# A post-norm decoder layer on one core: VectorE's order inside a round of the token-expert stage

## The chip, the cores and the metric

The kernel runs on one core of a Trainium2 chip as one launch. Its time is the device time in microseconds, and the lower is the better. A core has TensorE (matrix products and transposes, results in PSUM), VectorE, ScalarE, GpSimd, and SyncE, which here only issues transfers. Each engine works through a queue of its own; they meet at semaphores. In the profile PE is TensorE, PEld its weight loads, DVE VectorE, ACT ScalarE and POOL GpSimd.

## The reference

B = 4 sequences of S = 256 tokens with D = 256 features, 1024 tokens in all. Three blocks, each followed by a residual sum and a layer norm without scale or bias:

```python
x = _layernorm(x + attention(x))          # 16 heads, causal
x = _layernorm(x + xattn(x, itok, ctx))   # expert picked by the token's number
x = _layernorm(x + ffn(x))                # expert picked by a router, 4 x 1024 hidden features

def xattn(x, ids, W):                     # ctx_2048 is Wg, Wu and Wd at once: 4 matrices of 256 x 256
    e = minimum(clip(ids, 0, 12499) // 3125, 3)
    g = silu(x @ W[e].T); u = x @ W[e].T
    return (g * u) @ W[e].T

def layernorm(x): return (x - mean(x)) / sqrt(var(x) + 1e-5)
```

The change lies in the middle block. Since Wg and Wu are one matrix there, one projection z serves both: h = silu(z) z.

## The kernel before, in words

Matrix products keep nearly full float32 accuracy with three float16 products each: every operand is split into a high part (ScalarE rounds it to float16) and a low part (VectorE subtracts the high part from the original). `three` (L1099 to L1104) issues high by high, high by low and low by high for each slice of 128 features, so a product with 256 features takes six matmuls.

After attention, GpSimd scatters the 1024 normalised rows into a table in main memory sorted by expert. The four groups are padded to whole tiles of 128 rows, NS = 11 tiles in all, and SyncE loads the tiles back into `XS`. The token-expert stage then goes over them. It is a software pipeline written out by hand: all engines run through rounds s = 0, 1, 2, ..., and in round s each engine does its step for a different tile. These are the steps, with the tile each is for in round s:

- tile s: TensorE transposes the rows (L1322), ScalarE copies the high part (L595), VectorE makes the low part (L977, the first low part).
- tile s-1: TensorE makes the gate projection z (`three`, PSUM bank 2), ScalarE takes silu (L602), VectorE multiplies it by z (L991, the gate product, into `hh`).
- tile s-2: TensorE transposes h (L1341), ScalarE copies the high part (L608), VectorE makes the low part (L999, the second low part).
- tile s-3: TensorE makes the down projection (`three`, banks 4 and 7 in turn), VectorE adds the residual (L984, into `res`), takes the statistics (L995) and from them mean and variance (L1003, the means). GpSimd then adds epsilon (L443) and takes the power -0.5 (L444, into `rstd`).
- tile s-4: VectorE normalises the row (L1007, into `X2`).
- tiles s-5 and s-6: TensorE transposes `X2` (L1358), ScalarE copies it (L615), and TensorE computes the router's four logits (L1368).

TensorE's order in a round is: transpose of tile s, gate projection, transpose of h, down projection, transpose of `X2`, logits. The gate projection in round s waits for the first low part of tile s-1 and for the gate product of tile s-2, both VectorE's work of round s-1. The transpose of h also waits for the second low part of the tile before, and the down projection waits for its own second low part. Every wait is a semaphore count: `a2lo` for the first low part, `h2` for the gate product, `h2lo` for the second low part, `y2` for the down projection, `mv2` for the means, `rs2` for `rstd`, `x2_rdy` for the normalised row.

Rounds 0 to 10 take in a tile; rounds 11 to 16 drain the pipeline. The router works in two parts, tiles 0 to 6 and 7 to 10. At the start of round 13 VectorE's work for the first part is in front of the round's steps (`logits`, `top_expert`), at the start of round 14 the rest of it (`top_weight`, `places`), which ends with the rows' positions in a second sorted table (L778). From then on GpSimd scatters the eleven tiles (L451), and the last stage, the routed experts, begins when all are written. That stage has the same pair of means (L1051) and normalisation (L1056) with GpSimd's two steps between them (L457, L459).

ScalarE and VectorE also split weights for the last stage. In every second round from round 3 ScalarE takes one such chunk before its other steps (L480), so round 3 cannot start before that chunk's transfer has landed.

Of the kernel before, what the change touches and what calls it, by code (L numbers as in the profile page):

```python
# [13 lines left out]
ALU, ACT, AX = mybir.AluOpType, mybir.ActivationFunctionType, mybir.AxisListType  # L14

P = 128
B, S, D = 4, 256, 256
# [7 lines left out]
NS = NT + E - 1  # L25
# [34 lines left out]
def build(nc, x_tok, xT, ids, wqkvT, woT, ctxT, Wr, br, Wf, out):  # L60
    ctx = ExitStack()
    with ctx:
# [57 lines left out]
        mv = sb("mv", [P, 2, 2], F32)  # L120
# [42 lines left out]
        X2 = carve([NS, ROW], F32)  # L163
# [511 lines left out]
        def _(dve):  # L675
# [290 lines left out]
            for s in range(NS + 6):  # L966

                for part, (_, last) in enumerate(PARTS[:-1]):
                    if s == last + 6:
                        logits(part)  # L970
                        top_expert(part)
                    elif s == last + 7:
                        top_weight(part)
                        places(part)
                if s < NS:
                    dve.wait_ge(a2hi, s + 1)
                    v.tensor_tensor(a_lo[s % 2], ps[:, 0, 0:D].rearrange("p (k t) -> p k t", k=NK),  # L977
                                    a_hi[s % 2], ALU.subtract).then_inc(a2lo, 1)
                j = s - 3
                if 0 <= j < NS:  # L980
                    dve.wait_ge(y2, j + 1)
                    if j >= 2:
                        dve.wait_ge(x2_rdy, j - 1)
                    v.scalar_tensor_tensor(out=res[j % 2], in0=ps[:, (4, 7)[j % 2], 0:D], scalar=inv,  # L984
                                           in1=XS[:, j, 0:D], op0=ALU.mult, op1=ALU.add).then_inc(r2, 1)
                i = s - 1
                if 0 <= i < NS:
                    dve.wait_ge(sg2, i + 1)
                    if i >= 1:
                        dve.wait_ge(h2T, i)  # L990
                    v.scalar_tensor_tensor(out=hh[:, 0:D], in0=ps[:, 2, 0:D], scalar=inv, in1=sg[:, 0:D],  # L991
                                           op0=ALU.mult, op1=ALU.mult).then_inc(h2, 1)
                if 0 <= j < NS:
                    dve.wait_ge(r2, j + 1)
                    v.bn_stats(st[:, j % 2, :], res[j % 2]).then_inc(bn2, 1)  # L995
                i = s - 2
# [4 lines left out]
                if 0 <= j < NS:  # L1001
                    dve.wait_ge(bn2, j + 1)
                    v.bn_aggr(mv[:, j % 2, :], st[:, j % 2, :]).then_inc(mv2, 1)  # L1003
                i = s - 4
                if 0 <= i < NS:
                    dve.wait_ge(rs2, i + 1)
                    v.tensor_scalar(X2[:, i, 0:D], res[i % 2], mv[:, i % 2, 0:1], rstd[:, i % 2:i % 2 + 1],  # L1007
                                    ALU.subtract, ALU.mult).then_inc(x2_rdy, 1)

            last = len(PARTS) - 1  # L1010
            logits(last)
# [494 lines left out]
```

## Time and profile before

| | before |
|---|---|
| median of 3 runs | 321.65 us (321.32 to 321.87) |
| the profiled execution's own time | 322.61 us |
| its span, first to last instruction | 320.8 us |
| PE busy | 248.8 us, 78% of the span |
| DVE busy | 185.1 us, 58% |
| ACT busy | 130.3 us, 41% |
| POOL busy | 73.9 us, 23% |
| chain that ended last, by engine | PE 54%, DVE 16%, issue 9%, ACT 7%, DMA 5%, POOL 5% |

The shares are averages over stages with different limits. In time the span falls into attention (to about 131 us), the exchange of rows (to about 142 us), the token-expert stage (to about 186 us), the second exchange (to about 208 us) and the routed experts. "Idle before" in a row of a timeline is the time in which the engine did nothing before that instruction, and the releaser behind the arrow is what ended it. The duration of a row is of one instruction; neighbours on one engine overlap by some hundredths of a microsecond, so the distance from start to start is the cost of an instruction in a full queue.

### The profile page before, as it was taken

How to read it: one execution, taken by the hardware profiler on the slowest of the kernel's cores; microseconds unless marked ns; L12 is line 12 of the kernel's file. 1: busy time of each engine (PE TensorE's matmuls, PEld its weight loads, DVE VectorE, ACT ScalarE, POOL GpSimd, SP SyncE). 2: the span in 40 equal slices, each digit the busy share in tenths (PEclk: the TensorE clock that was granted, in tenths of full speed). 3: DMA queues.
4: the chain of work that ended last, by engine and by line, in shares of the span. 5: the costliest groups of instructions: out<-in, count | busy, mean ns of one | idle time of the engine just before them, and what ended most of it. 6: DMA issues, size and time to landing. Idle time of an engine off the chain costs nothing.

```text
span 320.8 us, 5861 instructions
## 1 busy us (share of the span) xinstructions
PE 248.8 (78%) x1991; PEld 165.2 (52%) x1992; DVE 185.1 (58%) x406; ACT 130.3 (41%) x218; POOL 73.9 (23%) x125
## 2 busy tenths in 40 slices
PE   4795789887986773447797537679999999999990
PEld 3364556555664551124676432236666656666570
DVE  3868577776889447813776758023544445455441
ACT  4451565855946674305575300033323213333210
POOL 8400000100141303810333268100222111222222
PEclk9799699999999998596999556599999999999997
DMA  6999072422253741448200011240000000000000
GB/s 201 339 326 284 6 261 68 127 73 67 68 164 84 215 133 39 191 144 298 102 3 0 2 42 68 89 115 2 16 18 1 2 11 16 16 16 16 9 13 2
DMA packets 18055, 29.29 MB, mean 91 GB/s; under 512 B 2796, under 2 KB 13550, under 8 KB 18032
## 3 DMA queue, kind: packets, MB, share of 16 engines
q1 hardware_dynamic: 16592, 25.81, 26.4%
q0 software_dynamic: 1440, 3.17, 2.7%
q8 instruction: 15, 0.25, 0.3%
q14 instruction: 8, 0.07, 0.1%
HBM read 19.69 MB, written 10.03 MB: 93 GB/s over the span
## 4 chain that ended last, share of the span: by engine, by line
PE 54%; DVE 16%; issue 9%; ACT 7%; DMA 5%; POOL 5%; SPq 3%; POOLq 0%; ACTq 0%; DVEq 0%
PE ps L1103 34%; DVE arena L848 3%; PE ps L1408 3%; ACT wf_hi L480 3%; PE ps L1213 2%; PE ps L1174 2%; PE ps L1109 2%; POOL sorted L422 2%; POOL sorted L451 2%; SPq L335 2%; DMA ring<-wqkvT 1%; PE ps L1170 1%; DVE wf_lo L686 1%; DVE arena L845 1%; DMA arena<-Wf 1%
## 5 line engine op out<-in xcount | busy, mean ns | idle before, releaser
L1103 PE MATMUL ps<-wf_hi,arena 128*128 x336 | 82.0, 329 | 2.8 <-DVE arena L1031 1.6
L1103 PE MATMUL ps<-wf_lo,arena 128*128 x168 | 55.2, 328 | 0.0
L1103 PEld LDWEIGHTS ps<-wf_hi,arena 128*128 128x128 f16 x336 | 32.8, 98 | 26.8 <-issue 6.7
L639 ACT ACTIVATE arena<-ps 128x512 f32<-128x512 f32 x22 | 13.2, 598 | 65.3 <-PE ps L1103 65.3
L1031 DVE SCALAR_TENSOR_TENSOR arena<-ps,arena 128x512 f32<-128x512 f32 x22 | 15.2, 692 | 25.3 <-ACT arena L639 13.5
L1109 PE MATMUL ps<-wf_hi,ones 128*128 128x512 f16 x51 | 18.9, 545 | 12.4 <-issue 6.1
L686 DVE SCALAR_TENSOR_TENSOR wf_lo<-ring,wf_hi 128x1024 f16<-128x1024 f32 x17 | 20.5, 1219 | 8.6 <-ACT wf_hi L480 8.6
L1103 PE MATMUL ps<-xT_hi,arena 128*128 x88 | 20.3, 295 | 5.4 <-DVE arena L991 4.6
L1103 PEld LDWEIGHTS ps<-wf_lo,arena 128*128 128x128 f16 x168 | 16.4, 98 | 9.4
L1103 PE MATMUL ps<-arena,xT_hi 128*128 128x512 f16 (+1 forms) x64 | 17.2, 358 | 4.9 <-DVE arena L805 2.3
L457 POOL TENSOR_SCALAR veps<-mv 128x1 f32<-128x1 f32 x11 | 2.5, 226 | 79.6 <-DVE mv L1051 79.6
L848 DVE TENSOR_REDUCE arena<-ps 128x4 f16<-128x1024 f32 x16 | 19.6, 1223 | 1.6 <-PE ps L1174 1.6
L480 ACT ACTIVATE wf_hi<-ring 128x1024 f16<-128x1024 f32 x17 | 17.8, 1061 | 5.2 <-DMA ring<-Wf 5.1
L1109 PEld LDWEIGHTS ps<-wf_hi,ones 128*128 128x128 f16 x51 | 6.5, 132 | 23.3 <-issue 15.3
L527 ACT ACTIVATE arena<-ps 128x1024 f32<-128x1024 f32 x16 | 16.6, 1039 | 0.9 <-PE ps L1197 0.7
L1193 PE MATMUL ps<-maskT,identB 128*128 128x512 bf16 x32 | 12.6, 395 | 4.3 <-DMA arena<-arena 4.3
L422 POOL DMA_INDIRECT sorted<-X,pos_i x8 | 14.1, 1762 | 7.0 <-DVE X L901 5.8
L1213 PE MATMUL ps<-arena 128*32 128x256 f32 (+1 forms) x256 | 13.7, 331 | 2.3 <-ACT arena L533 2.1
L461 POOL DMA_INDIRECT out<-arena,out_i x11 | 12.0, 1092 | 13.9 <-DVE arena L1056 13.9
L1045 DVE SCALAR_TENSOR_TENSOR arena<-ps,arena 128x256 f32<-128x256 f32 x11 | 5.3, 484 | 17.1 <-PE ps L1103 14.9
L414 POOL TENSOR_SCALAR veps<-mv 128x2 f32<-128x2 f32 x4 | 2.6, 640 | 53.9 <-DVE mv L894 53.9
L845 DVE TENSOR_REDUCE arena<-ps 128x4 f16<-128x512 f32 x16 | 11.0, 688 | 6.9 <-PE ps L1174 6.8
(202 smaller groups left out, 525.6 us busy)
## 6 DMA issues: line engine op xcount, KB each, us to landing
ring<-Wf SPq DMA_DIRECT2D x17, 512.0 KB, 3.8
sorted<-fill SPq DMA_DIRECT2D x1, 4515.0 KB, 22.0
arena<-Wf SPq DMA_DIRECT2D x7, 512.0 KB, 6.0
arena<-sorted SPq DMA_DIRECT2D x22, 129.0 KB, 2.1
sorted<-fill SPq DMA_DIRECT2D x1, 1419.0 KB, 7.2
ring<-xT SPq DMA_DIRECT2D x4, 256.0 KB, 5.5
X<-x_tok SPq DMA_DIRECT2D x1, 1024.0 KB, 8.4
ring<-ctxT SPq DMA_DIRECT2D x2, 512.0 KB, 3.9
```

The lines of the kernel that those rows point to most:

```text
L422: g.indirect_dma_start(sorted2[:, :], bass.IndirectOffsetOnAxis(ap=pos_i[:, tt:tt + 1], axis=0), X1[:, tt, :], None, bounds_check=NS * P - ...
L480: a.activation(chunk_dst(ORDER[n], True), src, ACT.Copy, scale=W_SCALE).then_inc(c_hi, 1)
L527: a.activation(Pf[n % 2][:, 1:3], ps[:, 4:6, :], ACT.Exp, scale=DK ** -0.5).then_inc(exped, 1)
L639: a.activation(sg[:, half * 512:(half + 1) * 512], ps[:, 2 * half, :], ACT.Silu, scale=1 / W_SCALE).then_inc(sg3, 1)
L686: v.scalar_tensor_tensor(out=chunk_dst(ORDER[n], False), in0=staged(n)[0], scalar=W_SCALE, in1=chunk_dst(ORDER[n], True), op0=ALU.mult, op ...
L845: v.tensor_reduce(dst[:, 0], ps[:, 0, :].rearrange("p (a k) -> p a k", a=G), AX.X, ALU.max, negate=True).then_inc(maxed, 1)
L848: v.tensor_reduce(dst[:, 1], ps[:, 1:3, :].rearrange("p c (a k) -> p a c k", a=G), AX.XY, ALU.max, negate=True).then_inc(maxed, 1)
L1031: v.scalar_tensor_tensor(out=hh[:, half * 512:(half + 1) * 512], in0=ps[:, 2 * half + 1, :], scalar=inv, in1=sg[:, half * 512:(half + 1) * ...
L1103: last = t.matmul(dst, xs(k), ws(k), start=(k == 0 and m == 0), stop=(k == nk - 1 and m == 2))
L1109: t.matmul(ps[:, bank, 0:moving.shape[-1]], ones[:, :], moving, start=True, stop=True)
L1193: t.matmul(ps[:, bank, :], identB[:, :], maskT[:, :, :].rearrange("p a k -> p (a k)"), start=True, stop=False)
L1213: last = t.matmul(ps[i * HEAD:(i + 1) * HEAD, 6, kt * P:S], Vs[:, TB * b + kt, at_:at_ + HEAD], q, start=kt == 0, stop=kt == TB - 1, tile_ ...
```

## The change

VectorE's steps of a round are issued in another order. Before: first low part (s), residual (s-3), gate product (s-1), statistics (s-3), second low part (s-2), means (s-3), normalise (s-4). After: normalise (s-4), first low part (s), gate product (s-1), residual (s-3), statistics (s-3), second low part (s-2), means (s-3). The router's blocks stay at the start of rounds 13 and 14, so the normalisation now comes behind them. All waits stay with their instructions, and no other engine's program changes.

```diff
--- before.py
+++ after.py
@@ -972,10 +972,22 @@
                     elif s == last + 7:
                         top_weight(part)
                         places(part)
+                i = s - 4
+                if 0 <= i < NS:
+                    dve.wait_ge(rs2, i + 1)
+                    v.tensor_scalar(X2[:, i, 0:D], res[i % 2], mv[:, i % 2, 0:1], rstd[:, i % 2:i % 2 + 1],
+                                    ALU.subtract, ALU.mult).then_inc(x2_rdy, 1)
                 if s < NS:
                     dve.wait_ge(a2hi, s + 1)
                     v.tensor_tensor(a_lo[s % 2], ps[:, 0, 0:D].rearrange("p (k t) -> p k t", k=NK),
                                     a_hi[s % 2], ALU.subtract).then_inc(a2lo, 1)
+                i = s - 1
+                if 0 <= i < NS:
+                    dve.wait_ge(sg2, i + 1)
+                    if i >= 1:
+                        dve.wait_ge(h2T, i)
+                    v.scalar_tensor_tensor(out=hh[:, 0:D], in0=ps[:, 2, 0:D], scalar=inv, in1=sg[:, 0:D],
+                                           op0=ALU.mult, op1=ALU.mult).then_inc(h2, 1)
                 j = s - 3
                 if 0 <= j < NS:
                     dve.wait_ge(y2, j + 1)
@@ -983,14 +995,6 @@
                         dve.wait_ge(x2_rdy, j - 1)
                     v.scalar_tensor_tensor(out=res[j % 2], in0=ps[:, (4, 7)[j % 2], 0:D], scalar=inv,
                                            in1=XS[:, j, 0:D], op0=ALU.mult, op1=ALU.add).then_inc(r2, 1)
-                i = s - 1
-                if 0 <= i < NS:
-                    dve.wait_ge(sg2, i + 1)
-                    if i >= 1:
-                        dve.wait_ge(h2T, i)
-                    v.scalar_tensor_tensor(out=hh[:, 0:D], in0=ps[:, 2, 0:D], scalar=inv, in1=sg[:, 0:D],
-                                           op0=ALU.mult, op1=ALU.mult).then_inc(h2, 1)
-                if 0 <= j < NS:
                     dve.wait_ge(r2, j + 1)
                     v.bn_stats(st[:, j % 2, :], res[j % 2]).then_inc(bn2, 1)
                 i = s - 2
@@ -1001,11 +1005,6 @@
                 if 0 <= j < NS:
                     dve.wait_ge(bn2, j + 1)
                     v.bn_aggr(mv[:, j % 2, :], st[:, j % 2, :]).then_inc(mv2, 1)
-                i = s - 4
-                if 0 <= i < NS:
-                    dve.wait_ge(rs2, i + 1)
-                    v.tensor_scalar(X2[:, i, 0:D], res[i % 2], mv[:, i % 2, 0:1], rstd[:, i % 2:i % 2 + 1],
-                                    ALU.subtract, ALU.mult).then_inc(x2_rdy, 1)
 
             last = len(PARTS) - 1
             logits(last)
```

VectorE's queue in two even rounds of the stage, before, from the means of one round to the means of the next. `arena` is the memory in which all the tiles of the stage lie, `ps` is PSUM, `mv` the means and variances, `st` the statistics.

```order
L1003 BN_AGGR mv<-st 128x2 [waits bn2]
L1007 TENSOR_SCALAR arena<-arena,mv,rstd 128x256 [waits rs2]
L977 TENSOR_TENSOR arena<-ps,arena 128x256 [waits a2hi]
L984 SCALAR_TENSOR_TENSOR arena<-ps,arena 128x256 [waits x2_rdy,y2]
L991 SCALAR_TENSOR_TENSOR arena<-ps,arena 128x256 [waits h2T,sg2]
L995 BN_STATS st<-arena 128x6 [waits r2]
L999 TENSOR_TENSOR arena<-ps,arena 128x256 [waits h2hi]
L1003 BN_AGGR mv<-st 128x2 [waits bn2]
```

The same stretch now, with the line numbers of the changed kernel.

```order
L1007 BN_AGGR mv<-st 128x2 [waits bn2]
L978 TENSOR_SCALAR arena<-arena,mv,rstd 128x256 [waits rs2]
L982 TENSOR_TENSOR arena<-ps,arena 128x256 [waits a2hi]
L989 SCALAR_TENSOR_TENSOR arena<-ps,arena 128x256 [waits h2T,sg2]
L996 SCALAR_TENSOR_TENSOR arena<-ps,arena 128x256 [waits x2_rdy,y2]
L999 BN_STATS st<-arena 128x6 [waits r2]
L1003 TENSOR_TENSOR arena<-ps,arena 128x256 [waits h2hi]
L1007 BN_AGGR mv<-st 128x2 [waits bn2]
```

The normalisation stood behind the means of the same round and now opens the next round; gate product and residual have changed places, and the statistics are next to the residual.

VectorE's queue at the start of round 13, before: the end of the router's first block (`logits`, `top_expert`), then the round's steps.

```order
L744 TENSOR_SCALAR ohf<-lg 128x28 [waits lg_sb]
L745 SCALAR_TENSOR_TENSOR where<-reset_e,ohf 128x28 [waits link_v]
L748 SCALAR_TENSOR_TENSOR ohf<-where,ohf 128x28 [waits link_v]
L750 TENSOR_TENSOR oh<-ohf,valid 128x28 [waits link_v]
L984 SCALAR_TENSOR_TENSOR arena<-ps,arena 128x256 [waits x2_rdy,y2]
L995 BN_STATS st<-arena 128x6 [waits r2]
L1003 BN_AGGR mv<-st 128x2 [waits bn2]
L1007 TENSOR_SCALAR arena<-arena,mv,rstd 128x256 [waits rs2]
```

And now:

```order
L744 TENSOR_SCALAR ohf<-lg 128x28 [waits lg_sb]
L745 SCALAR_TENSOR_TENSOR where<-reset_e,ohf 128x28 [waits link_v]
L748 SCALAR_TENSOR_TENSOR ohf<-where,ohf 128x28 [waits link_v]
L750 TENSOR_TENSOR oh<-ohf,valid 128x28 [waits link_v]
L978 TENSOR_SCALAR arena<-arena,mv,rstd 128x256 [waits rs2]
L996 SCALAR_TENSOR_TENSOR arena<-ps,arena 128x256 [waits x2_rdy,y2]
L999 BN_STATS st<-arena 128x6 [waits r2]
L1007 BN_AGGR mv<-st 128x2 [waits bn2]
```

The normalisation stands between the router's block and the round's residual, no longer behind the round's means.

## Rows read from the trace of the kernel before

**Rows 1.** TensorE's timeline, start of round 7: start and duration in us, engine, line, operation, count, [idle before <-releaser].

```profile
161.05 0.28 PE L1103 MATMUL ps<-xT_hi,arena 128*128 x1 [0.20 <-DVE arena L991]
```

**Rows 2.** VectorE's timeline: the last instructions of rounds 3, 4, 10, 12, the start of 13.

```profile
153.12 0.17 DVE L1003 BATCH_NORM_AGGREGATE mv<-st 128x2 f32<-128x6 f32 x1
...
155.94 0.39 DVE L1007 TENSOR_SCALAR arena<-arena,mv,rstd 128x256 f32<-128x256 f32 x1
156.24 0.42 DVE L977 TENSOR_TENSOR arena<-ps,arena 128x256 f16<-128x256 f32 x1
...
172.33 0.17 DVE L1003 BATCH_NORM_AGGREGATE mv<-st 128x2 f32<-128x6 f32 x1
...
176.44 0.42 DVE L984 SCALAR_TENSOR_TENSOR arena<-ps,arena 128x256 f32<-128x256 f32 x1 [0.86 <-PE ps L1103]
176.90 0.43 DVE L995 BATCH_NORM_STATS2 st<-arena 128x6 f32<-128x256 f32 x1
...
177.57 0.17 DVE L1003 BATCH_NORM_AGGREGATE mv<-st 128x2 f32<-128x6 f32 x1
...
177.95 0.17 DVE L731 TENSOR_SCALAR valid<-arena 128x7 f32<-128x7 f32 x1
...
179.55 0.42 DVE L984 SCALAR_TENSOR_TENSOR arena<-ps,arena 128x256 f32<-128x256 f32 x1
```

**Rows 3.** VectorE's timeline, round 6 of the token-expert stage.

```profile
160.04 0.42 DVE L984 SCALAR_TENSOR_TENSOR arena<-ps,arena 128x256 f32<-128x256 f32 x1 [0.61 <-PE ps L1103]
160.39 0.41 DVE L991 SCALAR_TENSOR_TENSOR arena<-ps,arena 128x256 f32<-128x256 f32 x1
160.72 0.42 DVE L995 BATCH_NORM_STATS2 st<-arena 128x6 f32<-128x256 f32 x1
161.05 0.41 DVE L999 TENSOR_TENSOR arena<-ps,arena 128x256 f16<-128x256 f32 x1
161.37 0.17 DVE L1003 BATCH_NORM_AGGREGATE mv<-st 128x2 f32<-128x6 f32 x1
161.46 0.38 DVE L1007 TENSOR_SCALAR arena<-arena,mv,rstd 128x256 f32<-128x256 f32 x1
```

**Rows 4.** GpSimd's timeline, the inverse deviation of round 6.

```profile
161.64 0.29 POOL L443 TENSOR_SCALAR veps<-mv 128x1 f32<-128x1 f32 x1 [1.80 <-DVE mv L1003]
...
162.01 0.57 POOL L444 TENSOR_TENSOR rstd<-veps,minus_half 128x1 f32<-128x1 f32 x1
```

**Rows 5.** The timelines of VectorE and GpSimd, the same steps in the last stage.

```profile
235.06 0.17 DVE L1051 BATCH_NORM_AGGREGATE mv<-st 128x2 f32<-128x6 f32 x1
...
235.33 0.23 POOL L457 TENSOR_SCALAR veps<-mv 128x1 f32<-128x1 f32 x1 [5.68 <-DVE mv L1051]
...
236.25 0.41 DVE L1056 TENSOR_SCALAR arena<-arena,mv,rstd 128x256 f32<-128x256 f32 x1 [1.01 <-POOL rstd L459]
```

**Rows 6.** The timelines of ScalarE and VectorE, attention stage, output's high and low part.

```profile
122.31 0.60 ACT L539 ACTIVATE arena<-ps 128x512 f16<-128x512 f32 x1 [2.83 <-PE ps L1237]
...
123.59 0.74 DVE L901 TENSOR_SCALAR X<-X,mv,rstd 128x256 f32<-128x256 f32 x2 [1.15 <-POOL rstd L415]
...
124.24 0.68 DVE L873 TENSOR_TENSOR arena<-ps,arena 128x512 f16<-128x512 f32 x1
```

**Rows 7.** The timelines of VectorE and GpSimd, positions and the first scatter.

```profile
184.42 0.17 DVE L778 TENSOR_TENSOR pos_i<-pos,off 128x7 int32<-128x7 f32 x1
...
185.44 1.09 POOL L451 DMA_INDIRECT sorted<-arena,pos_i  x1 [3.76 <-DVE pos_i L778]
```

**Rows 8.** View of windows: stretch, length, busy PE PEld DVE ACT POOL, granted clock, DMA share, GB/s.

```profile
158.00:171.00 13.00, 11.88 (x104) 10.38 (x105) 10.15 (x34) 8.06 (x21) 4.29 (x10) 1.00 0.01 2
...
178.00:186.00 8.00, 4.68 (x26) 4.25 (x24) 5.01 (x27) 2.28 (x4) 2.15 (x5) 0.50 0.01 3
```

**Rows 9.** TensorE's timeline, the drain of the stage.

```profile
175.34 0.41 PE L1341 MATMUL ps<-identF,arena 128*128 128x128 f32 x2 [1.03 <-DVE arena L999]
...
177.71 0.40 PE L1103 MATMUL ps<-xT_hi,arena 128*128 x1 [0.74 <-DVE arena L999]
```

## Prediction

> **What bounds the kernel now.** I read the shares and the slices of the page first, then the chain that ended last, then the timelines of VectorE, TensorE, ScalarE and GpSimd over the token-expert stage, and last the final stage, where the same helper work on GpSimd is waited for openly. The reader is to see three things.
>
> The stage with the changed order is the stretch from about 151 to 186 us. The chain runs almost unbroken through it, and in its even middle it is TensorE's work with one hole: the first matmul of the gate projection starts after 0.20 us of idle time that VectorE's gate product (L991) ends [rows 1]. From its start at 161.05 us the next round repeats 2.74 us later, so TensorE works 2.54 us a round. The period over seven rounds comes from the statistics' second half (the means, L1003): it starts at 153.12 us in round 3 and at 172.33 us in round 10 [rows 2], which is 19.21 us or 2.744 us a round. A round s is one pass of the loop; tile s enters it, and VectorE handles tiles s-1 to s-4 too.
>
> VectorE's own order in round 6 is residual, gate product, statistics, low part, means, normalise, and then the next round's first low part [rows 3]. Neighbours start 0.32 to 0.35 us apart and the means are followed by the normalisation after 0.09 us. With 0.30 us from normalisation to low part (155.94 to 156.24 us [rows 2]) and one more pitch to the residual the seven make 2.06 us of the 2.744, so about 0.68 us a round are idle; 0.61 us of it stand before this residual, which waits for the down projection. VectorE has slack and TensorE nearly has none.
>
> The normalisation needs the inverse standard deviation, which GpSimd computes from the means. That takes GpSimd two instructions: the means start at 161.37 us [rows 3], GpSimd's result ends at 162.01 + 0.57 = 162.58 us [rows 4], 1.21 us after. In the order before nobody sees this. L1007 in round s takes tile s-4, whose means were made a whole round earlier, so the result has been there for over a microsecond.
>
> **The change, part by part.** No instruction is added or removed; three things move inside a round.
>
> First, the normalisation of tile s-4 goes from the end of round s to its start. That looks like a small step, but the means of tile s-4 are the last instruction of round s-1. The two are now neighbours in VectorE's queue and the whole GpSimd trip lies between them. The final stage shows this very pair: means at 235.06, normalisation at 236.25 us, 1.01 us of it idle until GpSimd's rstd, with 0.23 us for GpSimd's first instruction [rows 5]. From means to normalisation I take 1.19 us. The other end is the 1.21 us above plus 0.03 us of signalling, 1.24 us. The lower end for the sum is 1.18 us, the row's rounding; below 0.80 us, GpSimd's 0.23 and 0.57 us [rows 4, 5] alone, it cannot be.
>
> What stands behind the waiting instruction matters more than the instruction. In the attention stage the row before shows it: ScalarE had finished the high part of the output (L539) at 122.31 + 0.60 = 122.91 us, but VectorE's matching low part L873 starts only at 124.24 us, behind a normalisation that waited 1.15 us for rstd until 123.59 us [rows 6]. The Trainium skill says the same of the engine (Perfetto Trace Analysis, "Per-engine timelines": VectorE, ScalarE and GpSimd are strictly first in, first out). Here the low part for TensorE's next gate projection, the gate product and the residual all queue behind the wait, and TensorE waits for the first two.
>
> Of the two trips the shorter one is the nearer case. GpSimd's first instruction takes 0.29 us in the token-expert stage, while a normalisation runs beside it from 161.46 us, and 0.23 us in the final stage, where VectorE is idle [rows 3 to 5]; the new order leaves VectorE idle as well. The Trainium skill (SBUF — State Buffer, "SBUF: two separate sides") says a VectorE instruction in a two-port mode locks a port pair that GpSimd needs. By that rule the trip is the one without contention, and without it the longer one, 0.05 us a round and 0.4 us in all more.
>
> Second, the gate product moves ahead of the residual. That takes the 0.20 us hole away in principle: the gate product no longer waits for the down projection. It is worth something only where VectorE arrives in time, and it does not.
>
> Third, the statistics now stand directly behind the residual they read. Before, the gate product lay between and the pair residual to statistics cost the usual pitch. Where it did not, in round 12, the statistics start 0.46 us after the residual (176.44 to 176.90 us) [rows 2], against a pitch of 0.33 us. So each round pays 0.13 us more. The bounds are 0.33 us (nothing) and 0.52 us, the same pair in the final stage, a shade dearer there; I take 0.46 us since it is the same instruction pair.
>
> The new round on VectorE, start to start: means to normalise 1.19, normalise to low part 0.30, low part to gate product 0.33, gate product to residual 0.33, residual to statistics 0.46, statistics to low part 0.33, low part to means 0.32 [rows 3]. The sum is 3.26 us, against 2.744 us. VectorE becomes the bound. Nothing else does: from a gate product, TensorE waits 0.66 us (160.39 to 161.05 us), then spends 2.54 us, less than the 3.26 us at hand, and the residual finds its projection done.
>
> The sum. Rounds 0 to 2 have neither normalisation nor statistics, and round 3 starts from a weight transfer that nothing here moves. Round 3: the statistics' 0.13 us, so its means stand at 153.25 us. Rounds 4 to 10: seven times 3.26 = 22.82 us, means of round 10 at 176.07 us instead of 172.33, that is +3.74. Rounds 11 and 12 lack the first low part, and 12 lacks the gate product: 1.19 + 0.30 + 0.33 + 0.46 + 0.33 + 0.32 = 2.93 us and 2.60 us, together 5.53 us where before it was 177.57 - 172.33 = 5.24 us, +0.29. The means of round 12 are 4.03 us late. From there on the wait is covered: in rounds 13 and 14 the router's block of small instructions now stands between the means and the normalisation: nine of them in round 13, 1.60 us from L731 at 177.95 to the residual at 179.55 us [rows 2], longer than the trip, and twelve in round 14. The router's first part follows from the last projections, so it is 4.0 us late as well.
>
> Is any of it given back behind the stage? The positions of the first part (L778, 184.42 us) release GpSimd's scatters, which start at 185.44 us [rows 7] and run back to back, eleven of them, until the last stage's loads may start. They have no slack in front, so the delay passes through whole. What follows is TensorE at full clock, shifted.
>
> The profiled execution took 322.61 us (span 320.8 us and 1.8 us around it), which is 0.96 us above the median of the three runs. With the change it would be 322.61 + 4.0 = 326.6 us; on the median, 321.65 + 4.0 = 325.7 us. Bounds of the known terms: with 0.33 and 1.18 us the even round is 3.12 us and the delay 7 x 0.376 + 0.0 = 2.7 us; with 0.52 us, taken as it stands, and 1.24 us it is 3.37 us, and 0.2 + 7 x 0.626 + 0.5 = 5.1 us.
>
> **Rivals.**
> *The clock falls.* The new round leaves TensorE idle for 3.26 - 2.54 = 0.72 us. It ran at full clock through rounds with idle time [rows 8], and fell only at 177.71 us, when of the 3.40 us behind it 1.77 us had been idle, gaps of 1.03 and 0.74 us [rows 9]. In the new round it works 78% of the time, so I expect the 2.4 GHz level up to round 11. If it fell to 1.2 GHz from round 4, a round would take at most 2 x 2.54 = 5.1 us, and over eight rounds the loss would grow to 19 us; if only from round 10, by 1 to 3 us more than forecast. Chance 0.08.
> *Part is given back.* The residual to statistics pair stays at the pitch, or the start of the last stage has play that the chain does not show. Then +1.0 to +2.7 us, 322.7 to 324.3 us. Chance 0.07.
> *The other side: the gate product sets the time.* If the inverse deviation came early enough, TensorE's hole would close: 0.20 us in four even rounds and up to 0.33 us, the distance by which the gate product moves, in the other four, together 2.1 us, 319.5 us. For it speaks that the gate product ends TensorE's wait in each of these rounds. It decides at one number: without the trip the round is 3.26 - 1.19 = 2.07 us, so the trip would have to cost under 2.744 - 2.07 = 0.67 us from means to normalisation. GpSimd's two instructions alone take 0.80 us. Chance 0.04.
> *It does nothing*, because VectorE's idle time swallows the wait. The wait adds 1.19 - 0.09 = 1.10 us a round and the idle time gives back 0.68, so this needs two fifths of the wait to be missing, and the statistics at their pitch. Within 0.64 us of no change: chance 0.03.
>
> **How the numbers follow.** The forecast case holds 0.78, with +2.7 to +5.1 us. The range takes it whole and the mild half of the clock case: 324.3 to 327.7 us. A measurement of this kernel tells 0.2%, or 0.64 us, from no change. Slower: 0.78 + 0.08 + 0.07 = 0.93; no change 0.03; faster 0.04.
>
> **What would show it.** Normalisation L978 idle for about 1.0 us, released by GpSimd, nine times in the stage (rounds 4 to 12), and the low part L982 and gate product L989 starting 0.3 and 0.63 us after it. Means L1007 every 3.26 us. TensorE's first gate matmul waiting about 0.4 us in each even round, for the gate product or the low part. Residual L996 without a wait for TensorE. The scatters starting 4 us later. The forecast is wrong if the means still come every 2.7 us, if the granted clock is 0.5 before round 11, or if the scatters shift by clearly less than the means of round 12.

## The result, and the profile after

| | before | after |
|---|---|---|
| median | 321.76 us (320.87 to 323.12, 6 runs) | 326.39 us (324.99 to 328.90, 6 runs) |
| ratio to before | | 1.0148, 95% interval 1.0117 to 1.0179 |
| the profiled execution's own time, span | 322.61, 320.8 us | 326.31, 324.5 us |

The change makes the kernel slower by 4.8 us (3.8 to 5.8), taken from the ratio. The forecast was 325.7 us, between 324.3 and 327.7 us. Ratios in this document leave out executions over 1.5% above the fastest of their kernel; the profiled one of norm_second below (326.76 us) is such a one, and only the length of its rounds is read.

The first view to read is the one that shows what VectorE waited for between 152 and 184 us: engine, line, what it waited for, us in total, times, longest.

```profile
DVE arena L978 <- POOL rstd L444: 9.0, 9, 1.0
```

In the trace of before this wait does not exist. It now stands nine times in the stage, once in each of rounds 4 to 12, at 1.0 us each. VectorE's timeline of round 7, from the means of round 6 to its own:

```profile
161.13 0.17 DVE L1007 BATCH_NORM_AGGREGATE mv<-st 128x2 f32<-128x6 f32 x1
162.30 0.41 DVE L978 TENSOR_SCALAR arena<-arena,mv,rstd 128x256 f32<-128x256 f32 x1 [1.00 <-POOL rstd L444]
162.63 0.42 DVE L982 TENSOR_TENSOR arena<-ps,arena 128x256 f16<-128x256 f32 x1
162.96 0.41 DVE L989 SCALAR_TENSOR_TENSOR arena<-ps,arena 128x256 f32<-128x256 f32 x1
163.29 0.41 DVE L996 SCALAR_TENSOR_TENSOR arena<-ps,arena 128x256 f32<-128x256 f32 x1
163.74 0.43 DVE L999 BATCH_NORM_STATS2 st<-arena 128x6 f32<-128x256 f32 x1
164.08 0.41 DVE L1003 TENSOR_TENSOR arena<-ps,arena 128x256 f16<-128x256 f32 x1
164.41 0.17 DVE L1007 BATCH_NORM_AGGREGATE mv<-st 128x2 f32<-128x6 f32 x1
```

It answers to [rows 3]. The normalisation (L978) comes 1.17 us after the means (L1007), with 1.00 us of idle time in front. Then first low part, gate product, residual, each 0.33 us on; the statistics 0.45 us behind the residual; second low part and means 0.34 and 0.33 us on. The round is 3.28 us long. The residual (L996) waits for nobody any more, where it waited 0.61 us for TensorE before. GpSimd in the same round, for [rows 4]:

```profile
161.39 0.22 POOL L443 TENSOR_SCALAR veps<-mv 128x1 f32<-128x1 f32 x1 [2.41 <-DVE mv L1007]
161.70 0.57 POOL L444 TENSOR_TENSOR rstd<-veps,minus_half 128x1 f32<-128x1 f32 x1
```

Its first instruction now takes 0.22 us instead of 0.29, as in the last stage [rows 5]. TensorE's timeline, for [rows 1]:

```profile
163.19 0.41 PE L1321 MATMUL ps<-identF,arena 128*128 128x128 f32 x2 [0.20 <-DVE arena L982]
163.62 0.28 PE L1102 MATMUL ps<-xT_hi,arena 128*128 x1
...
164.64 0.41 PE L1340 MATMUL ps<-identF,arena 128*128 128x128 f32 x2 [0.19 <-DVE arena L1003]
```

TensorE waits twice in this round for 0.2 us: with the transpose of the next tile for the first low part, with the transpose of h for the second. The gate projection behind the first one does not wait. The granted clock, for [rows 8]:

```profile
158.00:182.00 24.00, 19.54 (x153) 15.35 (x153) 15.77 (x51) 12.33 (x30) 6.33 (x16) 1.00 0.01 2
186.00:187.00 1.00, 0.00 (x0) 0.00 (x0) 0.46 (x4) 0.90 (x3) 0.67 (x2) 0.99 0.00 0
187.00:188.00 1.00, 0.00 (x0) 0.00 (x0) 0.90 (x6) 0.00 (x0) 0.12 (x1) 0.50 0.00 0
```

It is 1.00 (2.4 GHz) through rounds 12 and 13, although TensorE is busy only 19.5 of the first 24 us, and falls at about 187 us, in the router's block of round 14.

The marks of the stage, for [rows 2] and [rows 7]: the residual and the means of round 3, the means of rounds 10 and 12, the first instruction of the router's block in round 14, and GpSimd's first scatter.

```profile
153.42 0.42 DVE L996 SCALAR_TENSOR_TENSOR arena<-ps,arena 128x256 f32<-128x256 f32 x1 [0.35 <-PE ps L1102]
...
154.55 0.17 DVE L1007 BATCH_NORM_AGGREGATE mv<-st 128x2 f32<-128x6 f32 x1
...
177.52 0.17 DVE L1007 BATCH_NORM_AGGREGATE mv<-st 128x2 f32<-128x6 f32 x1
...
183.09 0.17 DVE L1007 BATCH_NORM_AGGREGATE mv<-st 128x2 f32<-128x6 f32 x1
...
186.67 0.17 DVE L757 TENSOR_SCALAR off<-valid 128x7 f32<-128x7 f32 x1 [0.51 <-ACT ex L580]
```

```profile
189.80 1.09 POOL L451 DMA_INDIRECT sorted<-arena,pos_i  x1 [2.68 <-DVE pos_i L778]
```

The same first instruction of the block in round 14, in the trace of before:

```profile
182.30 0.17 DVE L757 TENSOR_SCALAR off<-valid 128x7 f32<-128x7 f32 x1 [1.35 <-ACT ex L580]
```

From the means of round 3 to those of round 12 it is 28.54 us; before it was 177.57 - 153.12 = 24.45 us. That is +4.09 us in the place where the change acts. What stands ahead of and behind this stretch differs too, in both directions. The means of round 3 came 1.43 us later (154.55 against 153.12 us). Of this 0.86 us was there before any step of the stage: its first transpose waits for the rows' transfer in both, until 141.88 us before and 142.74 us after the change.

```profile
141.88 0.44 PE L1322 MATMUL ps<-identF,arena 128*128 128x128 f32 x2 [3.74 <-DMA arena<-sorted]
```

```profile
142.74 0.69 PE L1321 MATMUL ps<-identF,arena 128*128 128x128 f32 x2 [5.15 <-DMA arena<-sorted]
```

The other 0.57 us lies inside round 3: 0.44 us in front of the residual, which waited 0.35 us for a TensorE whose clock rose late (granted 0.50 from 150 to 152 us and 0.79 from 152 to 154 us, against 0.98 and 1.00 in the trace of before), and 0.13 us in the statistics. Between the means of round 12 and the router's block of round 14 the kernel took 3.58 us, against 182.30 - 177.57 = 4.73 us in the profile of before, so 1.15 us came back. The scatters start 189.80 - 185.44 = 4.36 us later, and so, within 0.1 us, does TensorE's first work of the last stage, ten matmuls that keep it busy:

```profile
202.93 4.45 PE L1109 MATMUL ps<-wf_hi,ones 128*128 128x512 f16 x10 [4.47 <-DMA sorted<-arena,pos_i]
```

```profile
207.22 4.12 PE L1108 MATMUL ps<-wf_hi,ones 128*128 128x512 f16 x10 [5.21 <-DMA sorted<-arena,pos_i]
```

The span is only 3.7 us longer. The rest came back in the opening of that stage: from these matmuls to TensorE's next long wait it took 13.07 us before (to 216.00 us) and 12.53 us after (to 219.75 us), and TensorE got its full clock earlier in the opening: the granted clock over the ten matmuls is 0.50 in the trace of before and 0.56 here. The traces of the experiments show how far such differences are the change's.

### The profile page after: what moved, and what is told of

Its sections match the earlier page's. It is cut to its first block, busy times and chain, and to the rows that moved or that the text cites. A ratio compares the mean times of both kernels' runs of the same rounds, so it can differ in the third digit from the quotient of the medians.

```text
span 324.5 us, 5861 instructions
## 1 busy us (share of the span) xinstructions
PE 249.4 (77%) x1991; PEld 164.1 (51%) x1992; DVE 186.2 (57%) x406; ACT 130.5 (40%) x218; POOL 74.2 (23%) x125
## 4 chain that ended last, share of the span: by engine, by line
PE 49%; DVE 20%; issue 9%; POOL 7%; ACT 7%; DMA 5%; SPq 2%; DVEq 0%; POOLq 0%; ACTq 0%
PE ps L1102 30%; DVE arena L848 3%; PE ps L1407 3%; ACT wf_hi L480 3%; POOL sorted L422 2%; PE ps L1212 2%; PE ps L1173 2%; POOL sorted L451 2%; POOL rstd L444 2%; PE ps L1108 2%; PE ps L1169 1%; DMA ring<-wqkvT 1%; DVE st L999 1%; DVE wf_lo L686 1%; DVE arena L845 1%
## 5 line engine op out<-in xcount | busy, mean ns | idle before, releaser
L1108 PE MATMUL ps<-wf_hi,ones 128*128 128x512 f16 x51 | 17.5, 513 | 13.0 <-issue 6.0
L480 ACT ACTIVATE wf_hi<-ring 128x1024 f16<-128x1024 f32 x17 | 17.8, 1061 | 5.3 <-DMA ring<-Wf 5.2
L422 POOL DMA_INDIRECT sorted<-X,pos_i x8 | 15.3, 1906 | 7.0 <-DVE X L901 5.8
L1173 PE MATMUL ps<-arena 128*128 128x128 f16 x144 | 13.2, 227 | 2.3 <-DVE arena L848 2.3
```

What stands on the lines that cost most here:

```text
L422: g.indirect_dma_start(sorted2[:, :], bass.IndirectOffsetOnAxis(ap=pos_i[:, tt:tt + 1], axis=0), X1[:, tt, :], None, bounds_check=NS * P - ...
L480: a.activation(chunk_dst(ORDER[n], True), src, ACT.Copy, scale=W_SCALE).then_inc(c_hi, 1)
L1108: t.matmul(ps[:, bank, 0:moving.shape[-1]], ones[:, :], moving, start=True, stop=True)
L1173: last = t.matmul(ps[:, bank, i * P:(i + 1) * P], q[:, h, qt * P:(qt + 1) * P], k[:, h // 2, kt * P:(kt + 1) * P], start=not diag, stop=(n ...
```

## The experiments

VectorE's steps of a round are named by letters here: n normalise, a first low part, g gate product, r residual, t statistics, h second low part, m means. Before is a r g t h m n, the change is n a g r t h m. Each kernel but the change itself (six runs of each, above) was timed in five rounds against the kernel before on the same chip. The even round below is a seventh of the distance between the means of rounds 3 and 10 in its profile, "3 to 12" the distance between the means of rounds 3 and 12, and "drain" that from the means of round 12 to the router's block of round 14. Where rounds alternate the even round is an average. In norm_third and long_trip the clock fell inside round 12 (0.78 from 177 to 178 us, 0.58 from 182 to 183 us), so their "3 to 12" holds some low clock.

| kernel | order, other edit | even round | 3 to 12 | drain | ratio to before, 95% |
|---|---|---|---|---|---|
| before | a r g t h m n | 2.744 | 24.45 | 4.73 | 1 |
| after | n a g r t h m | 3.281 | 28.54 | 3.58 | 1.0148 (1.0117 to 1.0179) |
| norm_first | n a r g t h m | 3.153 | 27.51 | 3.58 | 1.0092 (1.0059 to 1.0125) |
| norm_second | a n g r t h m | 2.954 | 26.25 | 4.73 | 1.0045 (1.0006 to 1.0084) |
| norm_third | a g n r t h m | 2.754 | 25.15 | 4.73 | 1.0016 (0.9988 to 1.0043) |
| norm_third_split | same, chunk later | 2.623 | 23.60 | 4.73 | 0.9967 (0.9934 to 1.0001) |
| gate_first | a g r t h m n | 2.590 | 23.17 | 3.58 | 0.9953 (0.9928 to 0.9979) |
| gate_split | same, chunk later | 2.457 | 22.12 | 4.72 | 0.9962 (0.9933 to 0.9991) |
| split_later | before, chunk later | 2.739 | 24.37 | 3.58 | 0.9965 (0.9935 to 0.9994) |
| full_split | after, chunk later | 3.284 | 28.55 | 4.73 | 1.0104 (1.0062 to 1.0146) |
| long_trip | after, longer trip | 3.574 | 31.59 | 4.72 | 1.0214 (1.0180 to 1.0247) |
| before_long_trip | before, longer trip | 2.747 | 24.47 | 3.58 | 1.0008 (0.9983 to 1.0034) |
| before_warm | before, extra matmuls | 2.759 | 24.50 | 3.59 | 0.9995 (0.9966 to 1.0024) |
| gate_split_warm | gate_split, extra matmuls | 2.457 | 22.12 | 3.58 | 0.9861 (0.9823 to 0.9899) |

**Only the normalisation (norm_first).**

```diff
+ normalise (s-4)                 # at the head of the round
  first low part (s); residual (s-3); gate product (s-1)
  statistics (s-3); second low part (s-2); means (s-3)
- normalise (s-4)
```

> Only the normalisation is moved to the head of the round; residual, gate product, statistics stay in the old order. Theory A (GpSimd's trip from the means to rstd now stands in front of everything in VectorE's queue): the wait of 1.00 us before the normalisation stays in rounds 4 to 12; the even round is 1.17 + 0.33 + 0.33 + 0.34 + 0.33 + 0.33 + 0.33 = 3.16 us against 2.74 us before and 3.28 us in the full change, so about +3.1 us against before and about 1 us less loss than the full change (the residual's direct successor is not its reader any more). Rival B (the swap of residual and gate product, with the statistics right behind the residual, makes the loss): within 0.5 us of before.

Measured: 1.0092, or +3.0 us, and an even round of 3.153 us. VectorE's means of round 5 and what follows:

```profile
159.83 0.17 DVE L1010 BATCH_NORM_AGGREGATE mv<-st 128x2 f32<-128x6 f32 x1
160.99 0.41 DVE L978 TENSOR_SCALAR arena<-arena,mv,rstd 128x256 f32<-128x256 f32 x1 [0.99 <-POOL rstd L444]
```

The normalisation's place alone makes 3.06 of the 4.09 us between rounds 3 and 12, and rival B falls. The full change pays 0.128 us more in each even round, in spite of the gate product's better place: there the statistics start 0.45 us behind the residual that they read, here 0.33 us behind the gate product.

**Only the swap (gate_first).**

```diff
  first low part (s)
+ gate product (s-1)
  residual (s-3)
- gate product (s-1)
```

> Only gate product and residual change places; the normalisation stays last. Theory A: TensorE's 0.20 us hole in front of the gate projection closes, the even round falls from 2.74 to about 2.54 us, VectorE has 2.19 us of work in it; 1 to 2 us faster than before. Rival B: slower than before by 2 us or more, since the statistics wait for the residual (0.46 instead of 0.33 us) and the residual comes later.

Measured: 0.9953, or -1.5 us (-2.3 to -0.7). The half of the change that was moved with the other is a gain by itself. But the expected even round was 2.54 us, and rounds 4 to 10 came out at 2.46 us, except rounds 7 and 9 at 2.91 and 2.92 us. ScalarE and VectorE at the start of a long one, round 7:

```profile
161.98 1.05 ACT L480 ACTIVATE wf_hi<-arena 128x1024 f16<-128x1024 f32 x1
162.93 0.37 ACT L595 ACTIVATE arena<-ps 128x256 f16<-128x256 f32 x1
```

```profile
162.29 0.38 DVE L1009 TENSOR_SCALAR arena<-arena,mv,rstd 128x256 f32<-128x256 f32 x1
163.33 0.42 DVE L977 TENSOR_TENSOR arena<-ps,arena 128x256 f16<-128x256 f32 x1 [0.66 <-ACT arena L595]
```

ScalarE's weight chunk (L480) stands in front of the high part (L595), and the first low part waits 0.66 us for it. Before, the same wait was 0.46 us and hidden by the residual's.

**Third place (norm_third), then with the chunk out of the way (norm_third_split).**

```diff
+ first low part (s); gate product (s-1)
  normalise (s-4)
- first low part (s); gate product (s-1)
  residual (s-3); ...
```

> The full change, but the normalisation stands third (first low part, gate product, normalise, residual, statistics, low part, means). Theory A: two instructions now run during GpSimd's trip, the wait shrinks from 1.00 to about 0.3 us, the round is 1.17 + 0.33 + 0.46 + 0.34 + 0.33 = 2.63 us, still VectorE's, about 0.8 us faster than before. Rival C (a wait for GpSimd costs a round its full length wherever it stands in it): as slow as the full change, +4 us.

Measured: 1.0016, no difference from before, where 0.8 us of gain was expected. Rival C (+4 us) falls. The waits of the stage name what was missed: rounds 4 to 10 are 2.61 to 2.64 us, except rounds 7 and 9 at 3.09 us, and these two start with

```profile
162.94 0.17 DVE L1010 BATCH_NORM_AGGREGATE mv<-st 128x2 f32<-128x6 f32 x1
163.92 0.42 DVE L977 TENSOR_TENSOR arena<-ps,arena 128x256 f16<-128x256 f32 x1 [0.80 <-ACT arena L595]
```

So the same chunk again. In the next kernel ScalarE takes it later:

```diff
-                if s >= 3 and s % 2 == 1 and n < NCH:
-                    split_hi(n)
-                    n += 1
                 if s < NS:
                     ... # high part of tile s
                 if 0 <= i < NS:
                     ... # silu of tile s-1
+                if s >= 3 and s % 2 == 1 and n < NCH:
+                    split_hi(n)
+                    n += 1
```

> The normalisation third, as in the run before, and ScalarE's weight chunk (L480) taken after silu instead of at the head of every second round. Theory E (the missed 0.8 us of the third place went to that chunk: rounds of 2.63 and 3.09 us in turn): all rounds 2.63 us, 1 to 2 us faster than before. Rival F (the long rounds come from the wait for GpSimd): rounds still alternate, no faster than before.

Measured: rounds of 2.61 to 2.64 us without exception, against 2.63 expected, and 0.9967 (interval to 1.0001), 1.6 us under the third place with the chunk in front. About 0.5 us of the 1.55 us between their two "3 to 12" is round 12, 3.12 us there at a falling clock and 2.62 us here. Theory E holds for the round; that it is faster than before is not clear of the measurement. What bounds the round takes a second look:

```profile
166.93 0.17 DVE L1010 BATCH_NORM_AGGREGATE mv<-st 128x2 f32<-128x6 f32 x1
167.02 0.39 DVE L977 TENSOR_TENSOR arena<-ps,arena 128x256 f16<-128x256 f32 x1
167.68 0.42 DVE L984 SCALAR_TENSOR_TENSOR arena<-ps,arena 128x256 f32<-128x256 f32 x1 [0.27 <-PE ps L1343]
168.10 0.41 DVE L989 TENSOR_SCALAR arena<-arena,mv,rstd 128x256 f32<-128x256 f32 x1
```

No idle time for GpSimd is shown here, and the gate product waits 0.27 us for TensorE. But the normalisation starts 1.17 us after the means, as in the first place, and 0.42 us after the gate product instead of 0.33 us: the trip still ends last, 0.09 us after the point at which a full queue would have started the normalisation.

**Second place (norm_second).**

```diff
+ first low part (s)
  normalise (s-4)
- first low part (s)
  gate product (s-1); residual (s-3); ...
```

> The full change with the normalisation second (first low part, normalise, gate product, residual, statistics, low part, means). Theory A: each instruction that goes ahead of the wait takes its own 0.33 us out of the round: 1.17 + 0.33 + 0.33 + 0.46 + 0.34 + 0.33 = 2.96 us, between 3.28 us (first) and 2.63 us (third), up to 0.14 us more in every second round for ScalarE's chunk; +1.5 to +2 us against before. Rival: the position makes no step, as slow as the full change (+4.6 us) or as fast as the third place (+0.5 us).

Measured: 1.0045, or +1.4 us (+0.2 to +2.7), an even round of 2.954 us. The wait behind one instruction:

```profile
159.89 0.41 DVE L982 TENSOR_SCALAR arena<-arena,mv,rstd 128x256 f32<-128x256 f32 x1 [0.70 <-POOL rstd L444]
```

In the rounds with a weight chunk the first low part waits 0.47 us for ScalarE instead, and the normalisation still starts 1.17 us after the means (164.62 and 165.79 us in one of them), so these rounds are no longer. First, second and third place give rounds of 3.28, 2.95 and 2.62 us, the last with the chunk out of the way. Each instruction in front of the normalisation takes its 0.33 us out of the round.

**A longer trip, in the new order and in the old (long_trip, before_long_trip).**

```diff
+                link(g.tensor_scalar(veps[...], mv[:, i % 2, 1:2], EPS, None, ALU.add))
                 link(g.tensor_scalar(veps[...], mv[:, i % 2, 1:2], EPS, None, ALU.add))
                 g.tensor_tensor(rstd[...], veps[...], minus_half[:, 0:1], ALU.pow).then_inc(rs2, 1)
```

> The full change with GpSimd's first instruction (add epsilon) done twice in each round of the stage, 0.30 us more from means to rstd, nothing else. Theory A: the trip lies on the path once a round in rounds 4 to 12, so 9 x 0.30 = 2.7 us slower than the full change, about +7.3 us against before, even round 3.58 us. Rival D (the loss comes from TensorE's or ScalarE's order against the new one, not from the trip): no difference from the full change, about +4.6 us.

> The kernel before with GpSimd's first instruction done twice in each round, 0.30 us more from means to rstd. Theory A: the normalisation comes a whole round later there, the trip has over 1 us of cover, no difference from before within 0.5 us. Rival D (a longer GpSimd step costs time in any order): +2 to +3 us.

Measured in the new order: an even round of 3.574 us, 0.293 us more than the change's 3.281, and 1.0214, which is 2.1 us above the full change's ratio (2.7 expected; the intervals allow it). The stretch from round 3 to 12 is 3.05 us longer than the full change's; nine times 0.293 us are 2.64 us of it, the rest is round 12 at a falling clock. VectorE's wait has grown by the same 0.29 us:

```profile
162.51 0.41 DVE L979 TENSOR_SCALAR arena<-arena,mv,rstd 128x256 f32<-128x256 f32 x1 [1.29 <-POOL rstd L445]
```

In the old order the same edit is worth nothing: 2.747 us a round, 1.0008. So it is not the trip that costs, but where the instruction that needs it stands. Rival D falls on both.

**The full change with the chunk later, and before with the chunk later (full_split, split_later).** The edit is that of norm_third_split.

> The full change with ScalarE's weight chunk taken after silu. If VectorE with the wait is the only bound of the round (theory A), ScalarE has cover and the round stays 3.28 us; only round 3 can start up to 1 us earlier, where the chunk's transfer held up the first high part. About +4 to +4.6 us against before. Rival: part of the loss was the chunk's, rounds under 3.2 us, +3 us or less.

> The kernel before with only ScalarE's chunk moved behind silu. The 0.46 us wait of the first low part in every second round has cover there (the down projection ends later), so the round stays 2.74 us: within 0.6 us of before, at most 1 us faster from the start of round 3. Rival: rounds of under 2.7 us, 1 us or more faster, and then the chunk alone was worth as much as the swap.

Measured: the even round stays at 3.284 and 2.739 us, so in neither does ScalarE's chunk set the round; in the full change VectorE with its wait is the only bound. The times are 1.0104, or +3.3 us (+2.0 to +4.7), and 0.9965, or -1.1 us (-2.1 to -0.2), each about 1.1 to 1.4 us under the kernel with the chunk in front, at the edge of what the intervals separate. A round 3 that need not wait for the chunk's transfer would do that, but the profiles do not bear it out. From the stage's first transpose to the means of round 3 it takes 11.54 to 12.24 us in the five kernels with the chunk later and 11.24 to 12.52 us in the nine with it in front. The cause stays open. The first transpose itself comes between 141.11 and 143.82 us over the fourteen profiles, before any step that the edits touch; so a difference of whole times between two single executions can hold up to 2.7 us that lie ahead of every edited step.

**The clock in the drain (before_warm).**

```diff
+                if s == NS + 1: keep_warm(4, wf_hi[:, 0:512], bank=0)
                 # transpose of h, s-2
                 ...
+                if s == NS + 2: keep_warm(3, wf_hi[:, 0:512], bank=0)
                 # down projection, s-3
```

> The kernel before, with four extra matmuls of 512 columns into an unused bank before the transpose of h in round 12 and three before the down projection in round 13; their product is never read. Theory G (1.2 us of the change's loss came back because TensorE was still at 2.4 GHz in round 13, where before it had fallen to 1.2 GHz): the drain stays at full clock, the router's first exponential comes about 1.2 us earlier, 321.76 - 1.2 = 320.6 us. Rival: the extra matmuls delay the drain by as much as the clock gives, no difference.

Measured: 0.9995, no difference. The drain column of the table says why the expectation was too simple. It has only two values, 3.58 and 4.73 us, and they follow the granted clock in round 13. The profile of before had 4.73, but before_long_trip, with the same work on TensorE, had 3.58, and the full change 3.58 while full_split, the same but for ScalarE's chunk, had 4.73. So in these kernels the clock of the drain falls in some executions and not in others, with gaps of the same size in front. Where it fell, they were 1.03 and 0.74 us before the transpose and the down projection [rows 9]. In before_long_trip they were the same, in the full change the last was 0.90 us, and the clock did not fall there:

```profile
175.32 0.41 PE L1344 MATMUL ps<-identF,arena 128*128 128x128 f32 x2 [1.03 <-DVE arena L1001]
177.69 0.28 PE L1106 MATMUL ps<-xT_hi,arena 128*128 x1 [0.74 <-DVE arena L1001]
```

```profile
183.23 0.28 PE L1102 MATMUL ps<-xT_hi,arena 128*128 x1 [0.90 <-DVE arena L1003]
```

Each kernel has one trace, so two drains of one and the same kernel were not seen; but the clock's mean over an execution differs within one kernel too, from 0.905 to 0.926 over 35 executions of before. Both kernels with the extra matmuls have 3.58 or 3.59, but so have five without them; that the extra matmuls hold the clock is not shown. The 1.15 us that the profile of the change seemed to give back was a difference between two executions, not a part of the change. The 0.54 us of the last stage's opening is of the same kind: it takes 12.07 us (norm_third) to 13.33 us (gate_first) over the fourteen profiles, 13.12 us in full_split, where VectorE's order is the change's.

**The best version (gate_split, gate_split_warm).** The swap, the chunk later, and then the extra matmuls.

> Only gate product and residual swapped, and the weight chunk taken after silu. Theory E: the rounds of 2.46 and 2.91 us of the run with the swap alone become 2.46 us each, 2 to 3 us faster than before. Rival: the chunk in its new place delays the high part of h by up to 0.5 us and with it the second low part, no gain over the swap alone (-1.5 us).

> Swap of gate product and residual, chunk behind silu, and the extra matmuls in rounds 12 and 13. The round is 2.46 us, and if the drain at 1.2 GHz took back 1.15 us in the run without the extra matmuls (4.72 us from the last even means to the exponential, against 3.58 us at full clock), this one is 1 us faster than that, about 2.3 us faster than before. Rival: the clock of the drain decides nothing in the timed runs, as the extra matmuls did nothing for the kernel before: -1.2 us.

Measured: gate_split has rounds of 2.457 us, as theory E has it, and "3 to 12" is 2.33 us less than before, but the ratio is 0.9962, only -1.2 us (-2.2 to -0.3) where -2 to -3 was expected. Its drain ran at the low clock in the profiled execution (4.72 us). With the extra matmuls the ratio is 0.9861, -4.5 us (-5.7 to -3.3): 318.96 us against 323.09 us on its chip. That is the fastest kernel of this study, and more than the traces explain. The granted clock from 171 to 178 us, first gate_split, then gate_split_warm:

```profile
171.00:178.00 7.00, 5.15 (x38) 4.49 (x35) 5.64 (x24) 2.24 (x6) 2.02 (x5) 0.79 0.01 2
```

```profile
171.00:178.00 7.00, 6.77 (x55) 5.00 (x55) 5.53 (x21) 3.56 (x8) 2.42 (x6) 1.00 0.00 0
```

The clock accounts for the drain's 1.14 us, and the last stage's opening is 0.86 us shorter in the second (12.21 against 13.07 us). The two profiled executions are only 0.35 us apart (320.00 and 319.65 us), since the stage began 2.07 us later in the second. The two ratios are 3.3 us apart, but the two medians only 1.7 us (320.65 and 318.96 us): they were measured on one chip at two times, and before itself had medians of 321.89 and 323.09 us there. Why, and how much of the 3.3 us is the kernel's, with five runs of it, stays open.

## Why the prediction was right

**The wait.** Nine waits of 1.0 us for GpSimd in rounds 4 to 12, released by rstd, as forecast; 1.17 us from means to normalisation against 1.19. The experiments show that it is the cause: norm_first has it without the rest, and long_trip and before_long_trip change the trip alone, with 0.293 us a round in one order and nothing in the other.

**The queue behind it.** That a waiting instruction holds everything behind it was read from [rows 6]. The three places of the normalisation show it in numbers: 3.28, 2.95 and, with the chunk later, 2.62 us.

**The swap.** Its gain was judged real but out of reach in the new order, at most 2.1 us alone. Alone it gives 1.5 us; it stops at ScalarE's chunk, which the prediction did not see, since the residual's wait hid it. With the chunk later the stretch from round 3 to 12 is 2.33 us shorter, more than the 2.1 us named as the most. The prediction took the whole round less one hole, 2.54 us, for TensorE's own work, and gate_split shows rounds of 2.457 us.

**The statistics beside the residual.** 0.13 us a round was forecast; 0.128 us is the distance of the full change's round from norm_first's. The Trainium skill (VectorE: DVE Perf Modes, "The DRAIN you can't avoid") says of eight copies in a row that a semaphore after each costs nothing extra. For the instructions here the rows show a cost: with a wait on its direct predecessor an instruction of 256 elements a partition starts 0.45 us behind it, without one 0.33 us.

**The sum.** Forecast 3.26 us a round, measured 3.281: normalise to low part took 0.33 us behind an idle engine, not the 0.30 us of a full queue. Between the means of rounds 3 and 12 the forecast has 22.82 + 5.53 = 28.35 us, measured 28.54. With the 0.13 us of round 3 the change's own part is +4.22 us by the profiles, where 4.03 was forecast. Forecast of the whole +4.0 us, measured +4.8 us (3.8 to 5.8); that the spans of the two profiles differ by nearly the forecast too (3.7 us) is partly luck, since four differences of +0.86, +0.44, -1.15 and -0.54 us, which as far as the other profiles show are not the change's, nearly cancel. One step of the bounds is miscounted: 7 x 0.376 us is 2.6 us, not 2.7; on the median that still gives 324.3 us.

**What was off.** TensorE's wait moved, but not where it was put: not 0.4 us at the gate projection but 0.2 us at each of two transposes. The sign that the text named for an error, scatters shifted by clearly less than the means of round 12, did appear: 4.36 us against 5.52 us. What differed was the clock of the drain between the two profiled executions, and the prediction had taken the drain to run alike in both. Behind the scatters the prediction has TensorE at full clock and the delay passed through whole. It did not hold in these two profiles: the last stage opens at 0.50 in the profile of before, and 0.54 us of the delay came back there. Round 3, too, was said to differ by the statistics alone, and came 1.43 us later for reasons that lie mostly in the stage's start. The rival of a clock that falls earlier did not come: TensorE was busy 81% of the time and kept 2.4 GHz.

## What to carry to other kernels

In a software pipeline written by hand, look at each pair that another engine stands between (here means, GpSimd, normalisation) and count what is queued between the two across the round's boundary, not inside one round. A step moved from the end of a round to the start of the same round is moved towards its producer by everything that stood between, and on an engine whose queue is strict it takes the whole round with it. Of a change with two halves, time each: here the swap alone was worth -1.5 us and the normalisation's place alone +3.0 us, and together they cost 4.8 us, more than their sum of 1.5, since the swap's gain needs the time that the wait takes, and its price, the statistics beside the residual, stays. A gain of one or two microseconds is better read between two marks of the stage than from the whole time, as long as the starts and the clock differ by that much from run to run; and it is worth looking where the clock stood between the marks.

## What was not expected of the hardware

- Two VectorE instructions of 128 x 256 float32 start 0.33 us apart, and 0.45 us when the second waits for the first's semaphore; that is 0.128 us a round in two kernels that differ in nothing else on that engine but the order of residual and gate product.
- With the same gaps in TensorE's work (1.03 and 0.74 us, in before and before_long_trip) the granted clock of the drain was 0.5 in one execution and 1.0 in the other; the drain took 3.58 to 3.59 or 4.72 to 4.73 us and nothing between, over fourteen profiled kernels, seven of each.
- TensorE kept the 2.4 GHz level for 24 us in which it was busy 19.5 us.
- GpSimd's addition on 128 x 1 took 0.29 us in the even rounds of before, where VectorE's normalisation ran beside it, and 0.22 us in those of the change, where VectorE was idle. In round 3 of before it took 0.23 us beside a first low part, which reads PSUM. The experiments did not test this apart.
